# Attention scores from rounded halves: three single passes in place of one float32 product

## The reference

```python
h = film(rmsnorm(x, norm1_w), cond, film1_w, film1_b)
Q = h @ q_w + q_b
K = h @ k_w + k_b
V = h @ v_w + v_b
scores = jnp.einsum('bnd,bmd->bnm', Q, K) * D ** (-0.5)
attn = jax.nn.softmax(scores, axis=-1)
out = jnp.einsum('bnm,bmd->bnd', attn, V)
x = x_in + (out @ proj_w + proj_b)
```

## Time and profile before

| what | value |
|---|---|
| median of 3 runs | 1821.47 us (1819.9 to 1822.71) |
| time of the profiled execution | 1819.76 us |
| its span in the trace | 1818.0 us |
| TensorE busy | 1806.6 us (99%) |
| VectorE, ScalarE, GpSimd busy | 1192.3, 865.0, 201.0 us |
| mean granted clock of TensorE | 0.987 |

### The profile page before, as it was taken

How to read it: one execution, slowest core, us unless ns; L and a number is a source line. 1 busy time by engine, 2 the same in 40 slices (tenths; PEclk the granted TensorE clock), 3 DMA queues, 4 the chain that set the end, 5 groups by cost and what they waited for, 6 DMA issues and landing times.

```text
span 1818.0 us, 23440 instructions
## 1 busy us (share of the span) xinstructions
PE 1806.6 (99%) x8606; PEld 1525.5 (84%) x8606; DVE 1192.3 (66%) x1551; ACT 865.0 (48%) x1450; POOL 201.0 (11%) x202
## 2 busy tenths in 40 slices
PE   8999999999999999999999999999999999999999
PEld 8888888888888888888888888888888888888887
DVE  4455656453664697488569748847875884786476
ACT  4435353544453555265345536535553553554344
POOL 0457677001000000000000000000000000000000
PEclk8999999999999999999999999999999999999999
DMA  7468686723216778667767866876786687677675
GB/s 287 128 219 306 232 304 226 248 100 116 60 67 206 204 237 278 189 191 265 247 200 235 278 195 190 274 244 190 248 281 180 193 280 234 191 239 243 194 227 198
DMA packets 199617, 391.87 MB, mean 216 GB/s; under 512 B 22864, under 2 KB 26960, under 8 KB 197456
## 3 DMA queue, kind: packets, MB, share of 16 engines
q1 hardware_dynamic: 199216, 390.11, 65.8%
q10 hardware_dynamic: 288, 0.26, 0.1%
HBM read 327.32 MB, written 62.98 MB: 215 GB/s over the span
## 4 chain that ended last, share of the span: by engine, by line
PE 98%; DMA 1%; ACT 1%; DVE 0%; issue 0%; SPq 0%; DVEq 0%
PE psum L653 34%; PE psum L673 22%; PE psum L551 14%; PE psum L681 11%; PE psum L586 3%; PE psum L587 3%; PE psum L622 3%; PE psum L591 3%; PE psum L631 2%; PE psum L565 1%; DMA norm_row<-rs_scratch 0%; PE psum L613 0%; DMA rs_scratch<-rstd 0%; ACT sq_attn L808 0%; ACT h L778 0%; DMA wkT_sb<-wkT_dram 0%
## 5 line engine op out<-in xcount | busy, mean ns | idle before, releaser
L653 PE MATMUL psum<-op_hi_P,ring 128*128 128x512 f32 x1792 | 561.8, 395 | 0.0
L673 PE MATMUL psum<-stage_hi,ring 128*128 128x512 f32 x1792 | 442.6, 389 | 0.0
L653 PEld LDWEIGHTS psum<-op_hi_P,ring 128*128 128x128 f32 x1792 | 341.4, 191 | 71.3
L673 PEld LDWEIGHTS psum<-stage_hi,ring 128*128 128x128 f32 x1792 | 336.4, 188 | 69.8
L653 PE MATMUL psum<-op_lo_P,ring 128*128 128x512 f32 x896 | 352.7, 394 | 0.0
L840 ACT CAST stage_hi<-x 128x1024 fp32r<-128x1024 f32 x224 | 235.4, 1054 | 235.2 <-PE psum L673 223.1
L1177 DVE TENSOR_TENSOR stage_lo<-x,stage_hi 128x1024 fp32r<-128x1024 f32 x224 | 273.4, 1224 | 72.3 <-ACT stage_hi L840 72.1
L824 ACT ACTIVATE x<-x,vecs 128x512 f32<-128x512 f32 x192 | 138.1, 723 | 328.4 <-DVE x L1164 328.3
L681 PE MATMUL psum<-stage_lo,ring 128*128 128x512 f32 x896 | 239.5, 389 | 0.0
L653 PEld LDWEIGHTS psum<-op_lo_P,ring 128*128 128x128 f32 x896 | 171.2, 191 | 36.1
L681 PEld LDWEIGHTS psum<-stage_lo,ring 128*128 128x128 f32 x896 | 168.2, 188 | 34.9
(11 more groups left out here) (140 smaller groups left out, 2242.9 us busy)
## 6 DMA issues: line engine op xcount, KB each, us to landing
ring<-wu_scratch SPq DMA_DIRECT2D x448, 256.0 KB, 3.0
ring<-wd_scratch SPq DMA_DIRECT2D x448, 256.0 KB, 2.9
x_tok<-x_dram SPq DMA_DIRECT2D x16, 1024.0 KB, 10.7
xT_in<-xT_dram SPq DMA_DIRECT2D x16, 1024.0 KB, 7.9
x2T_scratch<-xT_in SPq DMA_DIRECT2D x32, 512.0 KB, 3.4
hn<-x2T_scratch SPq DMA_DIRECT2D x32, 512.0 KB, 5.3
xres<-x2T_scratch SPq DMA_DIRECT2D x32, 512.0 KB, 5.3
out_dram<-xres SPq DMA_DIRECT2D x32, 512.0 KB, 4.3
```

Source lines behind the costliest of these rows:

```text
L653: mm = pe.matmul(to, wt, b, start=q in FRESH and t == 0, stop=t == len(steps) - 1, skip_group_check=True)
L673: mm = pe.matmul(bank(q, dt), a[:, dt, part, :], stage_hi[r][:, e, :], start=q in FRESH and ss == 0 and e == 0 and part == 0, stop=False, ...
```

## The change

g is no longer kept in float32. `keep_g` on ScalarE writes its rounded high half `g_hi`; a new step `g_low` on VectorE reads the same PSUM bank again, adds `wk_bq` and subtracts `g_hi`, and writes `g_lo`. Scores are made of three `float32r` passes for each chunk, over g_hi, g_lo, h_hi and h_lo. The `key_bias` product stays as it is. Both the next `v_product` on a bank and `scores` now wait for `g_low`. `g_lo` takes 8 KB per partition at 188, and `condT_sb` moves to 196.

```diff
-        g, v = at(72, "g", [P, KD, TOK]), at(80, "v", [P, GB, D])
+        g_hi, g_lo = at(72, "g_hi", [P, KD, TOK], F32R), at(188, "g_lo", [P, KD, TOK], F32R)
+        v = at(80, "v", [P, GB, D])
...
-        condT_sb = at(188, "condT_sb", [P, KD, B])
+        condT_sb = at(196, "condT_sb", [P, KD, B])
...
             def v_product(n, b):
                 p = n % 2
-                pe.wait_ge(g_read, GB * n + b + 1)
+                pe.wait_ge(g_lo_done, GB * n + b + 1)
...
             def scores(n):
-                pe.wait_ge(g_read, GB * n + GB)
+                pe.wait_ge(g_hi_done, GB * n + GB)
+                pe.wait_ge(g_lo_done, GB * n + GB)
                 pe.wait_ge(key_done, KD * n + KD)
                 wait_used(pe, exp_done, GB * n)
                 for b in range(GB):
                     product(score_b[:, b, :],
-                            [(g[:, k, tokens(b)], h[n % 2][:, k, tokens(b)]) for k in range(KD)]
+                            [t for k in range(KD) for t in split3(g_hi[:, k, tokens(b)], g_lo[:, k, tokens(b)],
+                                                                  h_hi[n % 2][:, k, tokens(b)],
+                                                                  h_lo[n % 2][:, k, tokens(b)])]
                             + [(key_bias[n % 2][:, tokens(b)], ones_r[:].bitcast(F32))], scored if b == GB - 1 else None)
...
             def keep_g(n, j):
                 act.wait_ge(g_full, GB * n + j + 1)
-                nc.scalar.activation(g[:, j, :], gv[j], ACT.Identity, bias=wk_bq[:, j:j + 1]).then_inc(g_read, 1)
+                nc.scalar.activation(g_hi[:, j, :], gv[j], ACT.Identity, bias=wk_bq[:, j:j + 1]).then_inc(g_hi_done, 1)
...
+            def g_low(n, j):
+                dve.wait_ge(g_hi_done, GB * n + j + 1)
+                dve.scalar_tensor_tensor(g_lo[:, j, :], gv[j], wk_bq[:, j:j + 1], g_hi[:, j, :].bitcast(F32), ALU.add,
+                                         ALU.subtract).then_inc(g_lo_done, 1)
...
             dve.wait_ge(bq_bk_done, 1)
+            for j in range(KD):
+                g_low(0, j)
             key_terms(0)
...
             for n in range(GROUPS):
                 if n > 0:
+                    g_low(n, 1)
                     add_output(n - 1, 2)
                     add_output(n - 1, 3)
+                    g_low(n, 2)
+                    g_low(n, 3)
                 if n < LAST:
                     wait_used(dve, scored, n)
                     scale_x(n + 1)
...
+                if n < LAST:
+                    g_low(n + 1, 0)
                 add_output(n, 0)
                 add_output(n, 1)
```

More of the change, by code:

```diff
@@ L247, in cond_block_kernel @@
             sem(n) for n in ("x_scaled", "h_done_dve", "h_done_act", "h_hi_done", "h_lo_done", "key_done"))
-        g_full, g_read, v_full, v_read, scored, top_done, bias_done, exp_done = (
-            sem(n) for n in ("g_full", "g_read", "v_full", "v_read", "scored", "top_done", "bias_done", "exp_done"))
+        g_full, g_hi_done, g_lo_done, v_full, v_read, scored, top_done, bias_done, exp_done = (
+            sem(n) for n in ("g_full", "g_hi_done", "g_lo_done", "v_full", "v_read", "scored", "top_done", "bias_done", "exp_done"))
         rden_done, probs_scaled, pT_full, pT_read, out_full, out_read = (
```

## The result

| | before | after |
|---|---|---|
| median | 1822.09 us | 1886.38 us (1884.32 to 1887.62) |
| span of the profiled execution | 1818.0 us | 1883.5 us |
| records of TensorE | 8606 | 8862 |
| mean granted clock | 0.987 | 0.982 |

The ratio is 1.036, 95% interval 1.0347 to 1.0373: slower by 64.3 us, where 28.5 us were forecast. The sign and the slots were right; 36 us more were lost elsewhere.

The account below looks back on a forecast made before the run. TensorE, busy for 99% of the span, was taken as the bound; extra `scores` slots add 28.5 us, all other terms nothing: 1819.8 + 28.5 = 1848.3 us, plus 1.7 us to the median, 1850.0 us; range 1845 to 1859 us.

Parts of the forecast that it names:

- What bounds it: Whole kernel: TensorE, busy for 99% of the span, goes from one instruction to the next in all 16 groups.
- the slot: TensorE in `scores`: each `float32r` pass of 128 columns takes 0.111 us, set by the weight load, not the columns.
- part 1: `scores`: 48 slots added, 32 removed per group, 1.78 us per group, 28.5 us over 16 groups, all on the path.
- The three rivals with another price of a pass: `scores`: columns alone, -13 us, chance 0.07; near 0.08 us, +5 us, 0.04; two slots, +114 us, 0.06.
- Part 2: `keep_g` writes a rounded value in place of float32: same shape, 0.69 us, nothing added.
- part 5: Start: four `g_low(0, j)`, 3 us, fall where VectorE waits 13.7 us for folded value weights; nothing added.
- part 6: Clock during the new passes in `scores`: 2.4 GHz expected to stay, nothing added.
- Part 3, `g_low`: VectorE: 64 operations of 0.749 us, 48 us in all, none on the path; 1.1 us left before `scores`.
- The room of 2.8 us before the maximum: VectorE: delayed `scale_x` and `modulate` end at 294.0, the maximum is wanted at 296.8, so in time.
- The rival "a new wait": `g_low` late for `scores` in every group, 1 us per group beyond the cover, +16 us, 1866 us; chance 0.05.
- Part 4, the last group: Last group, `mix_t4` and seven `operand_low` behind `g_low(15, 3)`: probabilities still in time by 2.8 us, nothing added.

Follow-up runs that it names:

- e3_passes_only: The change without `g_low` and its waits, the passes reading g_hi in place of g_lo: 1850.06 us, ratio 1.0159.
- e5_wide: `e1_h_first` with the passes of two of four sequences streaming 256 columns in place of 128: 1853.66 us, ratio 1.018.
- e1_h_first: The change, but VectorE runs the next group's `scale_x` and `modulate` ahead of `g_low(n, 2)` and `g_low(n, 3)`: 1849.46 us, ratio 1.0158.
- e2_pool_later: The change in its own VectorE order, but GpSimd's weight work waits until VectorE has modulated the next group's h: 1849.80 us, ratio 1.016.
- e8_late_h_only: The kernel before, plus one wait: VectorE begins the next group's `scale_x` only after `keep_g(n, 3)`: 1857.65 us, ratio 1.0194.
- e10_pool_halves: The change in its own order, each GpSimd weight operation cut into two of half the size: 1849.36 us, ratio 1.0157.

## Why the prediction was wrong

**What bounds it, the slot, part 1:** right. 256 more records, 0.112 us in `scores`, 0.113 by the time of `e3_passes_only`, and `e5_wide` shows that the columns don't set it, as the prediction reasoned; that the load does stays argued. The three rivals with another price of a pass are out.

**Part 2, part 5 and part 6:** right. `keep_g` takes 0.69 us, no new wait at the start, and the clock stays at 1.00 in `scores` where nothing else delays TensorE: in `e1_h_first` the groups are 32.1 us long without exception but those two that carry other work.

**Part 3, `g_low`:** its duration (0.749 us) and its cover were right; TensorE never waits for g_lo. The step that failed is the next one: "`scale_x` and `modulate` of the next group, which ran from 283.05 to 287.74 (4.7 us) and now from 289.3 to 294.0". The durations were carried from the old place to the new. In the old place GpSimd had just finished a batch of weight work and waited for the next load; in the new one the next batch is under way, and 4.7 became 13.0 us. The room of 2.8 us before the maximum (294.0 to 296.8) was right (3.0 in `e2_pool_later`) and was overrun, by 5.4 us in the group shown. `e8_late_h_only`, `e2_pool_later` and `e10_pool_halves` show each link of this.

The trace of before held the sign of it. Here are two of its rows that the prediction did not use: from the groups of VectorE between 91 and 335 us, and from the timeline of GpSimd in the group of the earlier trace rows.

```profile
L1003 DVE TENSOR_TENSOR h_lo<-h,h_hi 128x512 fp32r<-128x512 f32 x32 | 36.8, 1209 | 0.0
```

```profile
291.29 1.27 POOL L505 TENSOR_TENSOR w_sumP<-w_src 128x512 f32<-128x512 f32 x1 [7.95 <-DMA w_src<-w_dram]
```

`h_low`, which stood beside GpSimd's work, took 1.21 us on average, against 0.685 as its median over the whole run; and GpSimd was idle from 283.3 to 291.3 us, just while `scale_x` and `modulate` ran, and at work from 291.3 on, where the prediction put half of them. The rival "a new wait" had the kind right, a gap on top of the slots, but the wrong place, the wait for g_lo itself, and with +16 us less than half of the 36.

**How the loss is made up:** in the whole run TensorE waits 21 us more than before (16.3 for h_lo, 3.1 for probs, 1.0 each for h_hi and xT_in). The seven groups by themselves, as a window in the form of the earlier trace rows:

```profile
124.33:383.67 259.34, 236.78 (x1317) 202.56 (x1317) 204.84 (x232) 103.44 (x264) 143.08 (x129) 0.97 0.60 213
```

TensorE is idle for 259.34 - 236.78 = 22.6 us, and the granted clock is 0.97, where it is 1.00 in the same groups before: some 7 us. That is about 30 of their 34.6 us; some 5 us stay unassigned.

**Part 4, the last group:** right, no wait shows there; GpSimd is done by then.

## What to carry to other kernels

A step that is moved doesn't take its duration along. Before a VectorE step is put elsewhere, look at what GpSimd does in the new place, and price the VectorE instructions there by GpSimd's: here one of 0.34 us took some 1.45 beside an instruction of 1.29, and one of 0.68 took 1.77 beside one of 1.73. Many short ones lose the most, and one that reads PSUM may lose nothing (`g_low`). A product in rounded halves pays by the number of its passes, as long as they are short: with 128 streamed columns three passes cost three slots and the float32 product two, and a pass of 512 columns takes 0.227 us, so two slots for four times the columns. And before a small product is made cheaper, ask whether the result needs it.

## What the runs showed of the hardware

- A `float32r` pass costs 0.111 us with 128 columns, 0.12 with 256 and 0.227 with 512, at the 2.4 GHz level. A float32 product of 128 columns is two records of 0.111 us.
- `modulate` (128 x 128, one tensor operand in SBUF) goes from 0.34 to 1.13 us on average beside GpSimd's whole operations, in step with them (1.45 beside one of 1.29), and to 0.745 beside the halved ones (0.77 beside one of 0.73).
- `g_low`, which reads PSUM and SBUF, isn't slowed. After the change all 64 take 0.740 to 0.752 us, but none of them meets GpSimd's weight work; in `e2_pool_later` 14 do, and take 0.739 to 0.751 like the rest.
- Cutting GpSimd's operations in two costs the kernel nothing that can be measured (1849.36 us against 1849.46 in `e1_h_first`) and takes away a loss of 36 us that arises on another engine.
